# One attention head at a time over rings of three PSUM banks, and other places for the steps beside attention, beside the expert pairs and in the last stage

## The reference, cut to what matters

```python
x = layernorm(x + attn(x))       # softmax(q k^T / sqrt(8)) v, 16 heads of 8, rotary q and k
x = layernorm(x + moe(x))        # 16 experts of 64, 4 chosen of each token, and a shared expert
x = layernorm(x + linear_attn(x))# features elu(xR)+1, 32 for each head, kv = k'^T v, out = q' kv / norm
x = layernorm(x + lora_moe(x))   # x W^T + b, and 8 low-rank experts of rank 16, 2 chosen
```

## Time and profile before

| | us |
|---|---|
| median of 3 runs | 478.55 (477.23 to 478.7) |
| the profiled execution, its own time | 478.46 |
| its span | 476.4 |
| PE busy | 440.1 |
| DVE busy | 374.5 |
| ACT busy | 233.6 |
| POOL busy | 104.9 |

### The profile page before, as it was taken

The page is one execution under the profiler, slowest core; times in us unless marked ns, Lnnn a source line. Parts: engine busy times, 40 slices in busy tenths (PEclk is TensorE's granted clock), DMA queues, the critical chain, the costliest instruction groups (busy, mean ns, idle before and its releaser), DMA issues. The chain is left out here.

```text
span 476.4 us, 8304 instructions
## 1 busy us (share of the span) xinstructions
PE 440.1 (92%) x3049; PEld 223.3 (47%) x3085; DVE 374.5 (79%) x1000; ACT 233.6 (49%) x324; POOL 104.9 (22%) x103
## 2 busy tenths in 40 slices
PE   8789979999999999999799999998999999998783
PEld 3333323333432334333243456665766675675772
DVE  6299887889689888987986298869786897887466
ACT  2405646666676665675468612336335623634220
POOL 9891070800637000200002000210020022003012
PEclk9999989999999999999999999999999999999788
DMA  5765433122432024331003222321122112000001
GB/s 160 247 172 200 101 97 112 56 78 75 123 119 96 19 72 122 113 116 31 1 24 77 35 69 88 83 72 46 45 76 59 45 37 95 3 1 23 1 1 44
DMA packets 24867, 36.19 MB, mean 76 GB/s; under 512 B 2678, under 2 KB 16246, under 8 KB 24822
## 3 DMA queue, kind: packets, MB, share of 16 engines
q1 hardware_dynamic: 24828, 35.67, 25.8%
HBM read 23.94 MB, written 11.53 MB: 74 GB/s over the span
## 5 line engine op out<-in xcount | busy, mean ns | idle before, releaser
L1156 DVE TENSOR_REDUCE negmax<-psum 128x1 f32<-128x512 f32 x256 | 169.8, 688 | 36.5 <-PE psum L541 36.3
L854 ACT ACTIVATE probs<-psum 128x1024 f32<-128x1024 f32 x128 | 127.6, 1023 | 61.2 <-PE psum L557 55.2
L541 PE MATMUL psum<-KS,QS 125*128 125x512 bf16 x256 | 98.9, 387 | 8.3 <-DVE negmax L1156 4.7
L576 PE MATMUL psum<-probs,VA 128*32 128x256 f32 x1024 | 81.0, 392 | 0.4 <-ACT probs L854 0.4
L557 PE MATMUL psum<-QS,KS 128*128 128x512 bf16 x226 | 69.9, 382 | 2.4 <-ACT probs L854 0.4
L833 PE MATMUL psum<-xT,late 128*128 128x512 f32 x144 | 68.5, 598 | 1.4 <-DVE QS L1325 1.4
L541 PEld LDWEIGHTS psum<-KS,QS 125*128 125x128 bf16 x256 | 24.6, 96 | 82.7 <-DVE negmax L1156 38.5
L463 POOL TENSOR_SCALAR var<-mv 128x4 f32<-128x4 f32 x16 | 3.6, 227 | 246.2 <-DVE mv L1063 246.1
L986 ACT ACTIVATE QS<-psum 128x512 f32<-128x512 f32 x36 | 21.6, 599 | 50.6 <-PE psum L833 50.6
L820 PEld LDWEIGHTS psum<-late,QS 128*128 128x128 f32 x288 | 35.7, 191 | 14.2 <-issue 10.8
L1325 DVE SCALAR_TENSOR_TENSOR QS<-QS,psum 128x512 f32<-128x512 f32 x36 | 24.5, 679 | 20.9 <-ACT QS L986 20.9
(11 more groups left out here) (146 smaller groups left out, 546.9 us busy)
## 6 DMA issues: line engine op xcount, KB each, us to landing
stack_dram<-parts SPq DMA_DIRECT2D x24, 384.0 KB, 3.6
cw<-w_dram SPq DMA_DIRECT2D x32, 256.0 KB, 3.2
KS<-stack_dram SPq DMA_DIRECT2D x16, 288.0 KB
QS<-stack_dram SPq DMA_DIRECT2D x16, 288.0 KB
late<-in_late SPq DMA_DIRECT2D x6, 330.5 KB, 4.6
res<-in_x SPq DMA_DIRECT2D x4, 256.0 KB, 3.6
w_dram<-wT SPq DMA_DIRECT2D x4, 256.0 KB, 4.3
out_y<-KS SPq DMA_DIRECT2D x4, 256.0 KB, 2.4
```

The lines of the kernel that those rows point to most:

```text
L541: mm(sm_bank(u)[:, :], QS[b % 2][0:KROW, h, qt * P:(qt + 1) * P], KS[b % 2][0:KROW, h, :], start=True, stop=True).then_inc(sm_full, 1)
L576: last_ = mm(ps[6][32 * j:32 * j + 32, q], VA[b % 2][:, kt, h, :], probs[:, n % 2, j, q], start=(kt == 0 and half == 0), stop=(kt == NT - ...
L854: fn(probs[:, n % 2, 2 * hf:2 * hf + 2, :], psum[:, 2 * hf:2 * hf + 2, :], ACT.Exp, scale=float(DH) ** -0.5).then_inc(exp_done, 1)
L1156: V.tensor_reduce(out=negmax[:, G % 4, i:i + 1], in_=sm_bank(u)[:, :], axis=X, op=ALU.max, negate=True).then_inc(sm_free, 1)
```

## The change

`scores` and `exps` take one head at a time, 256 of each in place of 128 pairs, over a ring of three banks (0, 1, 2). `scores_for_max` has a ring of three banks (3, 4, 5). `values(n)` is one group of four products of 512 columns, after the third head of the iteration. The semaphores' counts are adapted. The steps in the slots, beside the expert pairs and in the last stage stand in new tables (`SLOTS`, `LAST_SLOTS`, `FIRST`, `STEPS`, `TAIL`, `TAIL_BANK`), and `WARM` has other numbers. The computation is the same.

```diff
-WARM = {("x2T", 3): 2, ("x3T", 3): 8, ("ghT", 3): 8}
+WARM = {("x2T", 3): 2, ("x3T", 3): 13, ("ghT", 3): 2, ("O", 3): 4, ("AT", 3): 3, ("KT", 3): 1}
...
-            return ps[(4, 5, 0, 1, 2, 3)[u % 6] if u < HG * NT else 4 + u % 2]
+            return ps[(4, 5, 0, 1, 2, 3)[u % 6] if u < HG * NT else 3 + u % 3]
...
-                    pe.wait_ge(sm_free, u - 3 if u < HG * NT + 2 else u - 1)
+                    pe.wait_ge(sm_free, {16: 13, 17: 14, 18: 12}[u] if u < HG * NT + 3 else u - 2)
...
-                if w >= 2:
-                    pe.wait_ge(exp_done, w - 1)
-                for j in range(2):
-                    h = HG * (G % NG) + 2 * hf + j
-                    last_ = mm(ps[2 * hf + j][:, :], KS[b % 2][0:KROW + 3, h, kt * P:(kt + 1) * P],
-                               QS[b % 2][0:KROW + 3, h, :], start=True, stop=True)
-                last_.then_inc(s_full, 1)
+                if v >= 3:
+                    pe.wait_ge(exp_done, v - 2)
+                mm(ps[v % 3][:, :], KS[b % 2][0:KROW + 3, h, kt * P:(kt + 1) * P], QS[b % 2][0:KROW + 3, h, :],
+                   start=True, stop=True).then_inc(s_full, 1)
...
-                    last_ = mm(ps[6][32 * j:32 * j + 32, q], VA[b % 2][:, kt, h, :], probs[:, n % 2, j, q],
-                               start=(kt == 0 and half == 0), stop=(kt == NT - 1), tile_position=(0, 32 * j),
-                               skip_group_check=True)
+                    last_ = mm(ps[6][32 * j:32 * j + 32, :], VA[b % 2][:, kt, h, :], probs[:, n % 2, j, :],
+                               start=(kt == 0), stop=(kt == NT - 1), tile_position=(0, 32 * j), skip_group_check=True)
...
-                if 2 * n + 3 < HALVES:
-                    scores(2 * n + 3)
-                ahead()
-                values(n, 0)
-                ahead()
-                for s in slots[2 * n]:
-                    beside_pe(*s)
-                values(n, 1)
-                ahead()
-                if 2 * n + 4 < HALVES:
-                    scores(2 * n + 4)
-                ahead()
-                for s in slots[2 * n + 1]:
-                    beside_pe(*s)
+                for j in range(HG):
+                    if j == 3:
+                        values(n)
+                    if HG * n + 4 + j < SCORES:
+                        scores(HG * n + 4 + j)
+                    ahead()
+                    if j % 2:
+                        for s in slots[2 * n + j // 2]:
+                            beside_pe(*s)
...
-                fn(probs[:, n % 2, 2 * hf:2 * hf + 2, :], psum[:, 2 * hf:2 * hf + 2, :], ACT.Exp,
-                   scale=float(DH) ** -0.5).then_inc(exp_done, 1)
+                fn(probs[:, n % 2, j, :], ps[v % 3][:, :], ACT.Exp, scale=float(DH) ** -0.5).then_inc(exp_done, 1)
```

Of the tables: in the slots the second "rope" of a batch goes from place 16 to 18, its "store"s start at 11 in place of 18, and "norm" of batches 2 and 3 goes from 20 to 22 and 23. Beside the expert pairs the step "x2T" of each batch goes one pair later:

```diff
-        steps = ((0, "chunk", 0), (1, "norm1", 0), (3, "x2T", 0), (4, "kp", 0), (4, "qp", 0), (5, "K", 0),
+STEPS = ((0, "chunk", 0), (1, "norm1", 0), (4, "x2T", 0), (4, "kp", 0), (4, "V", 0), (4, "qp", 0), (5, "K", 0), (5, "K", 1),
```

More of the change, by code:

```diff
@@ new lines @@
+LAST_SLOTS = ((0, "gate", 0), (16, "combine", 0), (17, "gate", 1), (29, "combine", 1))
+FIRST = ((0, "gate", 2, 0), (1, "heads", 3, 0), (2, "heads", 3, 1), (3, "heads", 3, 2), (4, "heads", 3, 3),
+         (6, "attnT", 3, 0), (6, "proj", 3, 0), (8, "norm", 3, 0), (8, "combine", 2, 0), (11, "resT", 3, 0),
+         (11, "gate", 3, 0), (21, "combine", 3, 0))
+TAIL_BANK = {("O", 2): 4, ("x2T", 3): 4, ("AT", 2): 5, ("kp", 3): 4, ("Y1", 2): 6, ("qp", 3): 4, ("V", 3): 5, ("KV", 3): 1,
+             ("KT", 3): 5, ("O", 3): 1, ("x3T", 2): 4, ("lg", 2): 4, ("la", 2): 0, ("AT", 3): 7, ("Y1", 3): 3, ("ghT", 2): 4,
+             ("x3T", 3): 3, ("base", 2): 7, ("lg", 3): 5, ("la", 3): 0, ("base", 3): 6, ("ghT", 3): 4}
@@ L781, in _ @@
                 keep_warm(1)
[L782 to L783 removed]
+                if u in (START - 6, START - 5, START - 4, START - 2):
+                    scores((START - 6, START - 5, START - 4, START - 2).index(u))
             u_next = [START]
@@ L967, in _ @@
             beside_act("max", 0, 0)
-            for w in range(3):
-                exps(w)
+            for v in range(4):
+                exps(v)
             for n in range(HALVES // 2):
-                if 2 * n + 3 < HALVES:
-                    exps(2 * n + 3)
-                if n % NT == NT - 1:
-                    outputs(n // NT)
-                for s in slots[2 * n]:
-                    beside_act(*s)
-                if 2 * n + 4 < HALVES:
-                    exps(2 * n + 4)
-                for s in slots[2 * n + 1]:
-                    beside_act(*s)
+                for j in range(HG):
+                    if HG * n + 4 + j < SCORES:
+                        exps(HG * n + 4 + j)
+                    if j == 2 and n % NT == NT - 1:
+                        outputs(n // NT)
+                    if j % 2:
+                        for s in slots[2 * n + j // 2]:
+                            beside_act(*s)
             for i in range(NB * PAIRS):
```

104 lines of the change are left out of this document (45 added, 59 removed), and 13 rows, old and new, of tables (STEPS, TAIL, layer2, steps).

## The result

| | before | after |
|---|---|---|
| median, us | 478.62 (477.23 to 479.7, 4 runs) | 459.43 (457.72 to 462.07, 4 runs) |
| ratio, 95% interval | | 0.9605 [0.9545, 0.9666] |
| the profiled execution, its own time | 478.46 | 462.07 |
| its span | 476.4 | 460.2 |

The spread after is wider than before: it has 457.72 and 457.97 at a mean granted clock of 0.993, 460.89 at 0.989, and 462.07, the profiled one, at 0.983.

What follows compares the result with a forecast made beforehand. PE was taken to set the attention loop's pace. From 478.5 us, 9.3 for attention, 0.8 for the expert stage and 3.4 for the last stage were subtracted, giving 465.0 us, range 457 to 473.

Steps and rivals of the forecast that it cites:

- One group of `values`: Attention loop: one group in place of two saves PE 0.23 us in an iteration, 3.08 becoming 2.85.
- Room for it: Attention loop: DVE's 2.62 us and ACT's new time in an iteration must lie below PE's 2.85.
- the third bank: Attention, first nine iterations: DVE can work off two results during a group of `values`; 1.0 us gained.
- DVE becomes the bound: Rival, attention loop: DVE limits the pace and halves the attention gain, total 469 to 472 us; chance 0.17.
- Single heads: Attention: narrower exponentials cost ACT 0.16 us more an iteration; 0.7 us charged, in the last nine iterations.
- The rings of three scores: Attention: scores waiting for exponentials beside output copies and "rope" steps; 1.5 us charged, 5 as upper bound.
- The layout: One attention iteration laid out by measured distances: 0.29 us left before a score needs its bank, so PE doesn't wait.
- iterations 48 to 54: Attention, 219.65 to 248.50 us: 1.6 us by PE, but PE waits for DVE's routing; 1.0 us gain taken.
- Expert stage: Steps moved beside the expert pairs remove at most a 1.15 us wait; -0.8 us taken, bounds -2.5 and +1.
- Last stage: After the expert stage: zeros hold the clock up, -2.8 us, fewer zeros ahead of the last "ghT" -0.6; sum -3.4.
- the zeros between the halves: Last stage, "O" of batch 3: four products of zeros between its halves, booked as 0.9 us uncovered cost.
- more than forecast: Rival: DVE's waits nearly vanish, with the wait at 63.21 and the low clock behind it; 457 to 461 us; chance 0.11.

Runs made afterwards that it cites:

- e1_two_groups: The changed kernel with `values` again in two groups of 256 queries, the rings of three banks kept: 474.35 us, ratio 0.9889.
- e2_two_max_banks: The changed kernel with two banks in place of three for the scores for the maxima: 480.67 us, ratio 1.003.
- e4_old_zeros: The changed kernel with the numbers of products of zeros (`WARM`) of the kernel before: 463.82 us, ratio 0.9653.
- e10_both_back: The changed kernel with two groups of `values` and two banks for the maxima: 488.19 us, ratio 1.0176.
- e7_two_score_banks: The changed kernel with two banks for the scores and four for the maxima: 473.95 us, ratio 0.9896.
- e3_before_one_group: The kernel before with only `values` made one group of 512 queries, where its second half stood: 482.62 us, ratio 1.0043.
- e8_old_expert_steps: The changed kernel with the tables `FIRST` and `STEPS` of the kernel before: 460.23 us, ratio 0.9616.
- e5: The kernel before with only the new numbers of products of zeros: 475.94 us, ratio 0.9937.
- e9: The changed kernel without the four products of zeros between the halves of "O" of batch 3: 462.45 us, ratio 0.9632.
- e6_longer_start: The changed kernel with 56 in place of 42 products of zeros ahead of the first scores: 461.04 us, ratio 0.9604.

## Why the prediction was right, and where it was off

**One group of `values`.** Right in size: 0.23 us forecast, 0.24 measured against the kernel before (3.08 and 2.84) and 0.25 in e1_two_groups (3.09). The row of 16 instructions in the earlier trace rows was the right one to take.

**Room for it.** "DVE's 2.62 and ACT's new time must lie below 2.85" was true and not enough. The 2.62 was PE's pace and not DVE's need, which is 4 x 0.60 = 2.4; that error was harmless. The condition compares totals of an iteration. Whether DVE can do its work in time depends on how many finished products wait for it when the group begins, and that is the number of banks. This is the step that I sized wrongly: I booked the third bank with 1.0 us, in the first nine iterations only, and it is worth 20.6 in the loop at the same clock (e2_two_max_banks, 231.6 against 211.0): 4.6 in the first nine iterations (39.6 against the 35.0 of e4_old_zeros, both without a fall of the clock) and 14.3 in iterations 9 to 47, where I had booked nothing. That the sum came out near all the same was luck: the change had the bank. Had it had only two, I would have forecast 466 and been wrong by 15 us. Among the rivals I had "DVE becomes the bound", against the third bank as its cure, and priced it at 5 us of lost gain; without the bank the gain is lost not by half but whole. DVE isn't the bound there either: in e2 it is busy for 113.5 of the 142.9 us of iterations 9 to 47. PE and DVE wait for each other in turn. With the bank the rival doesn't come (112.39 of 128.56, 87%, where I had said 93).

**Single heads** I booked with ACT's extra time alone (0.7), and ACT did have the room: 0.49 us each. That the new order crowds the maxima's products together, 14 us with two banks (e10_both_back), I didn't see. The two terms that I missed have opposite signs.

**The rings of three scores.** The layout held: no PE wait in iterations without steps, and with one bank less the wait that it foretells appears (e7_two_score_banks). The 1.5 us that I charged for output copies and ropes did come, as 2.7 us of PE's waits for exponentials against 0.4 before, but other gains cover them: the four stretches together gave -14.1 with everything in them, against my -9.3. The largest part of the difference is iterations 48 to 54, where I allowed 1.0 of the 1.6 that PE could gain and 2.8 came. In the kernel before PE waits there 0.93 us for DVE ahead of the product of the routing step "gate" (223.47 us), and DVE then 1.88 for PE; in the changed kernel "gate" stands one place earlier and its product (210.46) has no wait. The two reductions that moved out of the stretch take another 2 x 0.60 = 1.2 us of work from DVE there. The single group has little to do with it: e1_two_groups takes 26.6 us there, e3_before_one_group 29.5. That the new places of the slots did this was not tried by itself.

**Expert stage.** -2.5 against -0.8. I had read the wait of 1.15 us rightly, and not asked what the new places do to the wait of 1.42 four pairs later, which goes too (e8_old_expert_steps brings both back).

**Last stage.** -3.4 against -3.4, and the split by e4 and e5 confirms that the clock made it. But one term was argued wrongly: the zeros between the halves are not a mere loss of 0.9 beside those ahead; without them the clock falls (e9).

**The rival "more than forecast"** has the right band and not the right reason. It wanted DVE's waits nearly gone and with them the wait at 63.21 and the low clock behind it. DVE still waits 31.0 us for PE, PE's wait stands at 64.62 with 1.61 us, and the clock falls at 65.3. (e4_old_zeros has the same wait, 1.60 us, and no fall.)

**Signs.** Of the signs that I had named, the distance of 2.84, the group of 1.00, the 256 exponentials and the clock behind "O" came. DVE's waiting for PE "well below 36.3" came in part (31.0). And one sign of being wrong came: the clock fell in a new place.

**Not foreseen:** that place, the start. In the profiled execution the first queries landed 3.16 us late for PE, with 6.8 us at 0.50. Four runs, one of them profiled, don't settle whether the others were spared this or another fall.

## What to carry to other kernels

Before a saved stretch of PE time is booked, count for each engine behind it how much finished work its buffers can hold, and compare that with the longest time in which PE gives it nothing; totals of an iteration hide this. Making one operation longer and giving its consumer one more buffer belong together. Here, in iterations 9 to 47, the longer group alone brought nothing (e3: 136.5 for 136.6), the third bank with single heads but two groups a loss of 3.9 (e1), and all together a gain of 8.0. And products of zeros against a falling clock are worth trying in the middle of a busy step of many small products as well, not only in front of a wait; what the rows show of the clock decides.

## What the hardware showed that I had not expected

The granted clock fell in stretches in which PE's records show no idle time at all. In e6_longer_start it is 0.50 from 368.6 to 375.4 us with PE busy 6.80 of 6.80, from 3.0 us into 32 products of 36 columns with a weight load each, and in other executions of kernels with the same code there it did not fall. Ahead of the same kind of step in the last stage, four products of 512 columns were not enough (the fall came 2.9 us into it), and with four more in its middle the clock held (e9 against the changed kernel). The same wait of 1.6 us behind which the clock fell in one execution left it up in another (the changed kernel and e4_old_zeros). Falls ahead of the end of PE's work came in lengths of 3.4, 6.8 and 10.2 us.
